# A graph network's rounds of block products: the last two and first two blocks of a round multiplied chunk by chunk, and one memset moved to VectorE

## What is computed

```python
x = _layernorm(x + L0(x))   # two GCN convolutions: h = relu(segment_sum((h @ W)[src] * norm, dst) + b)
x = _layernorm(x + L1(x))   # two SAGE convolutions: mean over sources @ Wl.T + bl + h @ Wr.T
x = _layernorm(x + L2(x))   # edge weights: concat(x, segment_sum(x[src] * w, dst)) @ W.T + b
x = _layernorm(x + L3(x))   # message MLP over edges with batch statistics, segment sum, node MLP
```

## Time and profile before

| | us |
|---|---|
| median of 3 runs | 3437.61 (3436.4 to 3441.92) |
| the profiled execution | 3440.58, its span 3438.8 |

### The profile page before, as it was taken

One profiled execution on the slowest core, in us unless ns is written; L12 is line 12 of the kernel. 1 busy time (PEld: TensorE's weight loads), 2 busy tenths in 40 slices (PEclk: granted clock), 3 DMA queues, 4 the chain that ended last, 5 costly groups with the idle time before them and its releaser, 6 DMA issues. The chain is left out here.

```text
span 3438.8 us, 66062 instructions
## 1 busy us (share of the span) xinstructions
PE 3081.9 (90%) x24666; PEld 2671.8 (78%) x24666; DVE 1753.6 (51%) x5401; ACT 1275.5 (37%) x2187; POOL 2246.9 (65%) x2215
## 2 busy tenths in 40 slices
PE   1699999999799989978999899868999999999996
PEld 0477777788588768867777777767999999999996
DVE  6999995243433324346676666445433333333334
ACT  4655553010200000014666665533543333333333
POOL 3465662776677576746777777616777777777772
PEclk9799999999899999977999999957877777766775
DMA  4355555787668767851122222222222222222221
GB/s 158 138 190 187 186 188 210 273 282 271 208 239 289 248 236 242 282 159 36 44 45 49 46 45 48 46 81 76 46 46 45 45 45 45 46 45 45 46 45 42
DMA packets 162467, 433.61 MB, mean 126 GB/s; under 512 B 62937, under 2 KB 105090, under 8 KB 141798
## 3 DMA queue, kind: packets, MB, share of 16 engines
q1 hardware_dynamic: 91528, 303.37, 24.2%
q0 software_dynamic: 70624, 126.01, 15.9%
HBM read 335.70 MB, written 93.49 MB: 125 GB/s over the span
## 5 line engine op out<-in xcount | busy, mean ns | idle before, releaser
L1325 PE MATMUL ps<-arena 128*128 128x288 bf16 x7644 | 1100.3, 291 | 22.9 <-DVE arena L1108 22.9
L812 POOL DMA_INDIRECT work_all<-parts_dram,idx_all x768 | 820.3, 1068 | 355.1 <-issue 227.0
L1908 POOL DMA_INDIRECT arena<-table,idx_all x832 | 800.1, 962 | 290.2 <-issue 252.0
L1325 PEld LDWEIGHTS ps<-arena 128*128 128x128 bf16 x7644 | 765.0, 100 | 219.5 <-DVE arena L1108 18.7
L1453 POOL DMA_INDIRECT arena<-table,idx_all x512 | 517.2, 1010 | 172.8 <-issue 153.3
L2190 PE MATMUL ps<-M,arena 96*128 96x96 f32 x1664 | 438.3, 363 | 33.5 <-DVE arena L2074 30.9
L2190 PEld LDWEIGHTS ps<-M,arena 96*128 96x128 f32 x1664 | 330.7, 247 | 35.3 <-issue 32.3
L1204 PE MATMUL ps<-arena,spare 128*128 128x245 bf16 x975 | 291.7, 305 | 31.4 <-ACT arena L868 19.0
L2068 DVE COPY arena<-ps 80x1024 bf16<-80x1024 bf16 x104 | 71.5, 687 | 482.2 <-PE ps L2176 482.2
L2192 PE MATMUL ps<-arena 80*128 80x96 bf16 x2496 | 301.2, 240 | 0.0
L868 ACT ACTIVATE arena<-ps 128x980 bf16<-128x980 f32 x234 | 231.2, 991 | 165.6 <-PE ps L1204 165.6
(11 more groups left out here) (394 smaller groups left out, 5032.6 us busy)
## 6 DMA issues: line engine op xcount, KB each, us to landing
arena<-blocks_dram SPq DMA_DIRECT2D x117, 1568.0 KB
blocks_dram<-arena SPq DMA_DIRECT2D x39, 1568.0 KB, 5.7
arena<-table,idx_all POOLq DMA_INDIRECT x1344
parts_dram<-arena SPq DMA_DIRECT2D x28, 504.0 KB, 3.2
work_all<-parts_dram,idx_all POOLq DMA_INDIRECT x768
ea_dram<-arena SPq DMA_DIRECT2D x1, 4992.0 KB, 13.3
TAB<-ea_dram SPq DMA_DIRECT2D x13, 384.0 KB, 3.3
arena<-ea_dram SPq DMA_DIRECT2D x1, 4992.0 KB, 14.6
```

What stands on the lines that cost most here:

```text
L812: eng.indirect_dma_start(out=gat_rows[kk % 3][:, u, :], out_offset=None, in_=parts_dram[:, :], in_offset=bass.IndirectOffsetOnAxis(ap=idx_ ...
L1325: last = nc.tensor.matmul(apply_ps[n % 2], blk[m % 3][:, b, :], Hs[:, b, :], start=b == 0, stop=b == NB - 1)
L1908: eng.indirect_dma_start(out=rows[g % NROW][:, u, :], out_offset=None, in_=table[:, :], in_offset=bass.IndirectOffsetOnAxis(ap=idx_all[:, ...
```

## The change

The last two units of a round become blocks (the spots of the gathered groups are drawn together by one block). In rounds 2 and 3 these two blocks are multiplied together, seven matmuls of one and seven of the other (`last_pair`); behind each pair of sevens `chunk_free` rises, and `hi` of that chunk of the next round may overwrite `Hs`. ScalarE, VectorE and GpSimd take up the split of the next rows in between; the seventh chunk's remainder is made by VectorE (`last_rem`). The first two blocks of rounds 2 to 4 are multiplied together too (`first_pair`): the first 3 or 5 chunks of one, the same of the other, then by turns as the chunks come. SP stores the first three chunks ahead of the loads of the second and third block. GpSimd waits for the last gathered unit, not for the last unit. The memset of `aggT` at the end of round 4 goes from GpSimd to the end of the chain of small VectorE operations in the next block of code (the counts of `k_link` rise by one with it).

```diff
-        spots = [3.0 + k * (NBLK - 3.4) / (NGATH - 1) for k in range(NGATH)]
+        spots = [3.0 + k * (NBLK - 4.4) / (NGATH - 1) for k in range(NGATH)]
+        PAIRED = range(2, ROUNDS - 1)
@@ sync
                 for r in range(2, ROUNDS):
-                    for g in range(3):
+                    load((r - 1) * NBLK)
+                    for c in range(3 if r > 2 else 0):
+                        store_parts((r - 1) * NCH + c)
+                    for g in range(1, 3):
                         load((r - 1) * NBLK + g)
-                    for c in range(NCH):
+                    for c in range(3 if r > 2 else 0, NCH):
                         store_parts((r - 1) * NCH + c)
@@ gpsimd
                     if r < ROUNDS - 1:
-                        eng.wait_ge(applied, r * NU)
-                        for c in range(NCH):
+                        eng.wait_ge(applied, gather_end(r * NGATH - 1))
+                        for c in range(NCH - (r in PAIRED)):
                             rem(r * NCH + c)
...
-                eng.wait_ge(prod, (ROUNDS - 1) * NCH)
-                nc.gpsimd.memset(aggT[:, :], 0.0).then_inc(zeroed, 1)
@@ scalar, hi(n)
-                    if c == 0 and n:
-                        eng.wait_ge(applied, block_end(n // NCH * NBLK - 1))
+                    if r in PAIRED and c < NCH - 1:
+                        eng.wait_ge(chunk_free, (r - 2) * (NCH - 1) + c + 1)
+                    elif r and c in (0, NCH - 1):
+                        eng.wait_ge(applied, block_end(r * NBLK - 1))
@@ scalar, the end of rounds 2 and 3 (squares and root in rounds 2 and 4 alone)
+                    squares, root of chunks 0 to 3
+                    hi 0, hi 1, mid 0, hi 2, mid 1
+                    squares, root of chunk 4
+                    hi 3, mid 2, hi 4, mid 3, mid 4
+                    squares, root of chunks 5 and 6
+                    hi 5, mid 5, hi 6, mid 6
@@ vector
+                def last_rem(n):
+                    r, b = n // NCH + 1, slice((NCH - 1) * CB, NCH * CB)
+                    eng.wait_ge(hi_up, n + 1)
+                    eng.wait_ge(rem_up, n)
+                    eng.wait_ge(parts_up, n - 1)
+                    nc.vector.tensor_tensor(rem3[n % 2], rows_of(r)[:, b, :], Hs[:, b, 0:F], ALU.subtract).then_inc(rem_up, 1)
...
+                        if r in PAIRED and p == NU - 2:
+                            into_nodes(n - 1)
+                            first(r, NEARLY - 1)
+                            low(r * NCH)
+                            low(r * NCH + 1)
+                            if r == 2:
+                                second_half(r, NEARLY - 1)
+                            low(r * NCH + 2)
+                            sums(n)
+                            continue
+                        if r in PAIRED and p == NU - 1:
+                            low(r * NCH + 3)
                         sums(n)
...
+                    if r in PAIRED:
+                        first(r, NCH - 2)
+                        low(r * NCH + 4)
+                        first(r, NCH - 1)
+                        if r == 2:
+                            second_half(r, NCH - 2)
+                            second_half(r, NCH - 1)
+                        low(r * NCH + NCH - 2)
+                        last_rem(r * NCH + NCH - 1)
+                        low(r * NCH + NCH - 1)
@@ tensor
+                def chunk(n, m, c):
+                    for b in range(c * CB, (c + 1) * CB):
+                        last = nc.tensor.matmul(apply_ps[n % 2], blk[m % 3][:, b, :], Hs[:, b, :], start=b == 0, stop=b == NB - 1)
+                    return last
+
+                def first_pair(r, n):
+                    m, ahead = (r - 1) * NBLK, 3 if r == 2 else NEARLY
...
+                    for c in range(ahead):
+                        eng.wait_ge(parts_up, (r - 1) * NCH + c + 1)
+                        chunk(n, m, c)
+                    eng.wait_ge(sums_up, n)
+                    block_in(m + 1)
+                    for c in range(ahead):
+                        chunk(n + 1, m + 1, c)
+                    for c in range(ahead, NCH):
+                        eng.wait_ge(parts_up, (r - 1) * NCH + c + 1)
+                        last = chunk(n, m, c)
+                        if c == NCH - 1:
+                            last.then_inc(applied, 1)
+                        last = chunk(n + 1, m + 1, c)
+                    last.then_inc(applied, 1)
+
+                def last_pair(r, n):
+                    m = r * NBLK - 2
+                    block_in(m)
+                    block_in(m + 1)
+                    for c in range(NCH):
+                        last = chunk(n, m, c)
+                        if c == NCH - 1:
+                            last.then_inc(applied, 1)
+                        if c == 0:
+                            place(n - 1)
+                            eng.wait_ge(sums_up, n)
+                        last = chunk(n + 1, m + 1, c)
+                        last.then_inc(applied if c == NCH - 1 else chunk_free, 1)
@@ vector, the next block of code
-                link = Chain(eng, k_link, 0, 11)
+                link = Chain(eng, k_link, 0, 12)
...
                 link(nc.vector.tensor_copy(wwin, ps6[:, 0:NVW * NVT]))
+                link(nc.vector.memset(aggT[:, :], 0.0))
```

More of the change, by code:

```diff
@@ L947, in _ @@
                         continue
-                    if r in (2, 4):
-                        for c in range(NEARLY):
+                    normed = r in (2, 4)
+                    if normed:
+                        for c in range(NEARLY - 1):
                             squares(r, c)
                             root(r, c)
-                    if r < ROUNDS - 1:
-                        for c in range(NEARLY):
-                            hi(r * NCH + c)
-                    for c in range(NCH):
-                        if r in (2, 4) and 2 <= c < 2 + NCH - NEARLY:
-                            squares(r, NEARLY + c - 2)
-                            root(r, NEARLY + c - 2)
-                        if r < ROUNDS - 1:
-                            if c >= NEARLY:
-                                hi(r * NCH + c)
+                    if r in PAIRED:
+                        hi(r * NCH)
+                        hi(r * NCH + 1)
+                        mid(r * NCH)
+                        hi(r * NCH + 2)
+                        mid(r * NCH + 1)
+                    if normed:
+                        squares(r, NEARLY - 1)
+                        root(r, NEARLY - 1)
+                    if r in PAIRED:
+                        for c in range(2, NEARLY - 1):
+                            hi(r * NCH + c + 1)
+                            mid(r * NCH + c)
+                        mid(r * NCH + NEARLY - 1)
+                    if normed:
+                        for c in range(NEARLY, NCH):
+                            squares(r, c)
+                            root(r, c)
+                    if r in PAIRED:
+                        for c in range(NEARLY, NCH):
+                            hi(r * NCH + c)
                             mid(r * NCH + c)
@@ L1160, in _ @@
                                 second_half(r, c)
-                        lows = list(range(r * NCH, (r + 1) * NCH)) if r < ROUNDS - 1 else []
                         first(r, NEARLY)
                         for c in range(NEARLY + 1, NCH):
-                            for n in lows[:2]:
-                                low(n)
-                            lows = lows[2:]
                             first(r, c)
                             second_half(r, c - 1)
-                        for n in lows[:2]:
-                            low(n)
                         second_half(r, NCH - 1)
-                        for n in lows[2:]:
-                            low(n)
                     elif r == 1:
@@ L1180, in _ @@
                         low(r * NCH + NCH - 1)
-                    else:
-                        lows = list(range(r * NCH, (r + 1) * NCH))
-                        for c in range(NEARLY, NCH):
-                            first(r, c)
-                            for n in lows[:2]:
-                                low(n)
-                            lows = lows[2:]
-                        for n in lows:
-                            low(n)
                     if r < ROUNDS - 1:
@@ L1308, in _ @@
                             eng.wait_ge(sums_up, n - 1)
-                        if is_block:
+                        if r > 1 and p == 0:
+                            first_pair(r, n)
+                        elif r in PAIRED and p == NU - 2:
+                            last_pair(r, n)
+                            continue
+                        elif (r > 1 and p == 1) or (r in PAIRED and p == NU - 1):
+                            pass
+                        elif is_block:
                             m = (r - 1) * NBLK + i
@@ L1318, in _ @@
                                 if p == 0 and b % CB == 0:
```

(1 more changed line is left out.)

20 lines of the change are left out of this document (12 added, 8 removed).

## The result

The changed kernel's median over ten runs is **3419.53 us** (3412.49 to 3435.07); the kernel before, on the same chip, took 3438.03 us over ten. The ratio is 0.9948, 95% interval 0.9926 to 0.997. The forecast was 3421.6. Two later sets gave the changed kernel 0.9964 (0.9943 to 0.9984) and 0.9947 (0.9927 to 0.9967). As differences of medians the three sets give 18.5, 13.9 and 18.8 us.

A forecast was written before the change was run, and what follows sets the result against it. The prediction took each new round to be bound by the start of its first gather, behind the row-splitting chain. Terms -5.8 + 1.5 - 4.4 - 7.9 + 0.6 = -16.0 us took 3437.6 to 3421.6 us; range 3412 to 3431.

The forecast's parts named there:

- The pair at the end of round 3: End of round 3: multiplying the last two blocks together lets splitting start earlier, moving round 4's first gather by -7.9 us.
- The pair's own term: End of round 2: multiplying the last two blocks together moves round 3's first gather by -4.4 us, despite later sums.
- The order of the units: Round 2: eight gathered groups one block earlier wait for late rows, +1.5 us, upper end 4.3; zero in other rounds.
- The memset: End of round 4: taking it off GpSimd frees a held VectorE operation, -5.8 us, bounds -6.0 and -5.0.
- the cover: Code after round 4: VectorE's memset fits beside TensorE's work with 0.8 us left, costing nothing; otherwise 0.6 us.
- My term for the clock: Starts of rounds: TensorE stands longer before its first two gathered groups and runs at the lower clock, +0.6 us.
- The gathers gate: Rounds 3 and 4: the first gather sets the round's clock, with the stray product still 28 us behind it.
- Pairs worth half: Rival, 0.17: port meetings and row landings at their upper bounds, total -7.2 us, 3430.4 us.
- The early release that does nothing: Rival, 0.05: some other wait holds the high parts to the pair's end, giving 3434 us.
- The serial queue: Rival, 0.05: in the pairs each chunk's four steps follow one another, holding both sums; total +10.5 us, 3448.1 us.
- Gathers that do not gate: Rival, 0.07: rows land quickly, so the end of blocks 0 and 1 counts; total -28.8 us, 3408.8 us.
- That the memset is not the cause: Rival, 0.06: the memset did not hold VectorE at the end of round 4; only pairs pay, -10.2 us, 3427.4 us.

The follow-up runs named there:

- e3: The changed kernel without the early release, so every high part again waits for the end of the last block: 3452.15 us, ratio 1.004 to the kernel before.
- e4: The changed kernel with the last two units' sums ahead of low part 3, in round 2 also of low part 2: 3423.31 us, ratio 0.9951 to before.
- e7: The changed kernel with the last two units' sums ahead of low parts and only the last two gathered groups moved: 3417.56 us, ratio 0.9954 to before.
- e12b: Second measurement of the changed kernel with sums ahead of low parts and only the last two gathered groups moved: 3418.64 us, ratio 0.9926 to before.
- e2: The kernel before with only the gathered groups drawn together by one block, no pairs and no moved memset: 3452.36 us, ratio 1.003.
- e6: The changed kernel with only the last two gathered groups of a round one block earlier, the others where they were before: 3417.42 us, ratio 0.995 to before.
- e1: The kernel before with only the memset of the weighted sums moved from GpSimd to VectorE: 3444.45 us, ratio 1.0013.
- e10b: Second measurement of the kernel before with only the memset of the weighted sums moved to VectorE: 3443.64 us, ratio 0.9996.
- e5: The changed kernel with the memset of the weighted sums back on GpSimd: 3425.0 us, ratio 0.9952 to the kernel before.
- e9b: The kernel before, nothing edited, measured and profiled again: 3443.92 us, ratio 0.9996.
- e8: The changed kernel, nothing edited, measured and profiled again: 3423.73 us, ratio 0.9964 to the kernel before.

## Why the prediction was right, and where it was wrong

The time was 2 us off, in part by luck: the terms were not all right. Means of the profiles in the table, changed less before, against the forecast:

| stage | forecast | measured |
|---|---|---|
| up to s2 | 0 | 608.3 - 611.7 = -3.4 |
| s2 to G3 (order +1.5, pair -4.4) | -2.9 | 282.9 - 282.2 = +0.7 |
| s3 to G4 (pair) | -7.9 | 283.8 - 291.5 = -7.7 |
| G to s, rounds 3 and 4 (clock) | +0.6 | -1.7 and +0.5 |
| s4 to N (memset) | -5.8 | 283.5 - 292.2 = -8.7, of it -5.9 behind the last products |
| N | -16.0 | 1512.9 - 1533.1 = -20.1 |

Gains that I had not foreseen, up to s2, from G3 to s3 and from s4 to the last products, hid a missed loss in round 2.

**The pair at the end of round 3** was -7.9, and from the end of the pair to G4 it measures -6.9, -7.1 and -7.8 (26.7 us before; 19.7, 19.6 and 18.8 changed). The largest of the three is the profile in which the last products took 3.37 us and not 6.0 to 6.2. The -7.7 of the stage has 0.3 us of the block behind the stray product in it, so the term was some 0.6 us too large. High parts begin at 1172.0 instead of behind the last block, the pair's queue gives the chunks in the order worked out, and G4 moves with the last low part. e3 shows that the release is what does it: without it the 19.7 us are 29.9.

**The pair and the order in round 2** were wrong together by 3.6 us. The pair's own term was -4.4 and measures -3.0 (pair end to G3, 31.8 to 28.9). Of the missing 1.4 us, some 0.3 is where I put the end of the last block, 0.3 the wait for the sums, and 0.8 lies behind the products' start (24.0 us to G3 where I had 23.2). The step "both sums stand behind low parts in VectorE's queue, ... start at 864.85" had the right wait, and the products did come 4.8 us behind the pair end where I had about 4.5. What I did not price is TensorE's clock: it pauses twice there, its granted clock over those products is about half, and 28 matmuls take 6.29 us instead of 3.37. The windows of the changed kernel (columns: stretch, its length, busy time of PE, PEld, DVE, ACT and POOL with counts, granted clock, DMA share, GB/s):

```profile
867.00:874.00 7.00, 6.63 (x31) 6.34 (x32) 3.04 (x6) 0.16 (x1) 0.00 (x0) 0.53 1.00 382
```

That is the lower of TensorE's two levels, 1.2 GHz. Only part reached G3, since first(5) needs 14 of the 28. e4 and e7 put the sums first and gain 3.1 and 4.4 us over the changed kernel in this stretch, so in round 2 the order of one queue was worth as much as the whole term. In e4 the 28 matmuls still take 5.98 us behind one short pause, in e7 and e12b 3.37: which pause costs the clock is not settled.

The order of the units was +1.5. The stage from s2 to the pair end grew by 1.6 to 4.9 us (251.9 to 255.2 against a mean of 250.3), and in the changed kernel TensorE's waits for rows in it went from 3.4 and 2.3 us to 5.6, 7.5 and 4.4: +3.0 in the mean, the rest is the block behind the stray product. The mechanism was right (eight groups a block early while gathers are issued without a pause, the wait of 1.69 us at 847.82 is one), and the size lay between my 1.5 and my upper end of 4.3. I had taken the low end for a row of 0.90 us. But that row was one group's wait, and five, eight and five groups wait in the stage (five and four before). With the order alone (e2) the waits are 3.8 us, and moving two groups and not eight leaves 4.1 to 4.9 (e6, e7, e12b), so what the eight cost by themselves is not well known.

**The memset** was -5.8 and measures -5.9, both where it is alone (e1, e10b) and in the changed kernel: last products to N is 22.58 and 22.59 us before, 16.63 to 16.67 in these five profiles. In the changed kernel 2.0 us of it come from the order and the rest from the memset: with the order changed and the memset on GpSimd (e2, e5) it is 20.5. It was right that it held that VectorE operation for its whole length. In four profiles the held operation ends 0.02 or 0.03 us after the memset (before 1519.77 and 1519.74, e9b 1522.50 and 1522.47, e2 1521.39 and 1521.37, e5 1508.66 and 1508.63), while tensor_tensor and tensor_reduce operations beside the same memset keep their 0.86 and 0.85 us. The Trainium skill (SBUF — State Buffer, Who interferes with whom) says that copies, casts and `tensor_scalar` can enter a mode that takes the port pair shared with GpSimd, that the first to issue then blocks the other entirely, and that a reduction never does so. The trace agrees on which operations are blocked and for how long. On who comes first it is less clear: in the profile before, the record of the blocked operation starts 0.57 us ahead of the memset's.

On the cover I was wrong by a little. I let the memset start right behind L1550's counterpart; there are 1.40 us between them that no wait explains. The cover is gone, and TensorE's product 1 comes 12.04 us behind N instead of 11.51, the 0.5 to 0.6 us that I had named for that case.

In the total the memset is open. e1 and e10b show no gain against before, and e5 none against e8. In e1 and e10b what lies behind N is 10.1 and 3.6 us longer than in the profiles of before and of e9b. Resampled, e10b less e9b is -0.3 us (-8.2 to +7.9) and e5 less e8 +1.3 (-8.7 to +10.6), which leaves room for the memset's 5.9 and 3.9 us. e1's interval (1.4 us less to 10.3 more) does not. I found no wait that takes the gain back, and it stays open whether there is one or the scatter of the gather stream hid the gain.

**The stages priced at nothing.** Up to s2 the changed kernel is 3.4 us ahead in the mean (607.5 to 609.4 against 610.0 and 613.5). This is not shown to be the change: e1 and e10b, which are the kernel before up to there, have s2 at 608.6 and 615.1. Between rounds 1 and 2, in the two profiles first compared, the last products run 3.37 instead of 4.32 us and the first 98 matmuls of round 2 12.17 instead of 13.62, so TensorE's granted clock was higher; e1 has 3.37 us too and e10b 4.78.

In round 4, s4 to the last products went from 269.3 and 269.9 us to 266.9. Of these 2.4 and 3.0 us, 2.0 and 2.6 are the block behind the stray product, 8.19 and 8.73 us before and 6.16 in all three profiles of the changed kernel; the last 0.4 comes with the order of the units (e2 has it). Before, TensorE stood 5.07 and 4.47 us right ahead of the stray product. In the changed kernel it has stood 5.97 us at the first gathered product already, the block behind that one is the slow one (7.71 us at 1219.31), and 2.2 us are left ahead of the stray product. That block lies ahead of s4, so its extra 1.5 us are in G4 to s4, which came out near 28 all the same. My term for the clock, +0.6, was for the stages from G to s alone. That the place of the long pause decides is argued, and no run moves it alone: e12b fits (3.78 us ahead of the stray product, then a block of 7.31), but e1 has 7.30 behind 1.59 us, so the length of the last pause is not all.

**The gathers gate.** In size this held in round 4 (28.4, 28.4, 27.8 us against the 28 forecast), and the longer waits came: 9.24 and 5.97 us at the first gathered product. But the last wait ahead of the stray product is now VectorE's in round 4 too (2.21 us, in place of 5.07 for the row), so that 28 came out again is in part luck. In round 3 the stray product came at G3 plus 25.7 to 26.9, which I had listed as a sign of being wrong. It is one in size only: the rows are still what TensorE waits for, but it waits once and not at the second group too, and the stray product then waits for VectorE and not for a transfer. The loads of the blocks are over by then:

```profile
890.00:905.00 15.00, 6.17 (x51) 4.72 (x48) 1.28 (x4) 0.00 (x0) 10.37 (x11) 0.77 0.98 382
905.00:914.00 9.00, 8.59 (x59) 6.44 (x60) 1.78 (x3) 0.00 (x0) 6.38 (x9) 0.81 0.22 51
```

That the loads end earlier because blocks 0 and 1 end earlier is argued, not tested.

Of the other signs, products 5 and 6 come 4.8 to 5.0 us behind the pair of round 2 instead of 1.6, so 3.3 to 3.4 us late and not over 5, and TensorE stands 0.33 us ahead of its product 1 in the next code, a gap that I had listed. One reading of mine was loose: in the 28.6 us at the end of round 2 TensorE is busy for 13.9 us by the rows; 9 is what that work takes at the upper clock.

**The rivals.** Pairs worth half would be -1.4 and -4.9 us; they measure -3.0 and -7.3. The early release that does nothing is refuted by e3. The serial queue is refuted for the changed kernel: low 3 held the second sum by 1.99 us, not 15. It is, though, what e3 became: with the parts late and the order kept, the sums wait 11.89 us and the kernel is slower than before. Gathers that do not gate are refuted by the 9.24 us. That the memset is not the cause is refuted for the stage and not for the total.

## What to carry to other kernels

When work moves ahead of the end of a stage, write out the queue of each engine that it enters and put what releases the critical engine first: two reductions of 0.45 us behind low parts cost TensorE 3.9 us of pauses, and in round 2 putting them first gave as much again as the pair had gained there (3.1 us). Then ask what ends last: in round 3 the same order gave nothing, for the stores came last there. Price a shift of many producers by the sum of waits over all of them, not by the tightest one. Look for the first block behind a long pause and take its extra time out before you compare stages: here it was up to 2.6 us, and 1.7 of the 2.6 us between the changed kernel's profiles from s3 to G4. Where a later stage scatters by 10 us from run to run, judge an edit by repeated profiles of its own stage and by timed sets side by side, and say so when only the first shows a gain.

## What was not expected of the hardware

- A 5.45 us memset on GpSimd, which reads nothing, stops a VectorE operation on seven elements per partition until it ends, whichever of them meets it: 6.05, 6.13, 4.07 and 4.07 us instead of 0.17.
- The VectorE memset of 96x6400 (5.39 us, as the earlier trace rows) starts 1.40 us after the instruction ahead of it with nothing to wait for (changed, e1, e10b); the 96x896 one, at 1190.35, follows within 0.14 us.
- At the end of round 3 the changed kernel's TensorE paused 1.71 us for the last sum in one profile and 1.72 in the third, and the 28 matmuls behind it took 6.15 us in the one and 3.37 in the other. The clock granted after one and the same pause differs between executions of one kernel.
- GpSimd's gather stream of 488 transfers had no stall in any profile and still took between 636.5 and 661.2 us.
